# First loads cut by k and cast on two engines, warm-ups on a constant, and rows added into two banks throughout the last pass

## The reference

```python
s = jnp.einsum('bn,hln->bhl', x, beta)
ssq = jnp.einsum('bn,hln->bhl', x * x, beta * beta)
fm = 0.5 * jnp.sum(s * s - ssq, axis=-1)
linear_out = x @ W.T + b
return fm + linear_out
```

## Time and profile before

| | us |
|---|---|
| median of 3 runs | 778.99 (777.09 to 779.22) |
| profiled execution, its own time | 776.45 |
| its span, first to last instruction | 774.7 |
| PE busy in the span | 770.4 |
| DVE busy in the span | 570.5 |

### The profile page before, as it was taken

How to read it: one execution, slowest core, us unless ns; L and a number is a source line. 1 busy time by engine, 2 the same in 40 slices (tenths; PEclk the granted TensorE clock), 3 DMA queues, 4 the chain that set the end, 5 groups by cost and what they waited for, 6 DMA issues and landing times.

```text
span 774.7 us, 9622 instructions
## 1 busy us (share of the span) xinstructions
PE 770.4 (99%) x3382; PEld 634.4 (82%) x3382; DVE 570.5 (74%) x582; ACT 395.9 (51%) x503; POOL 343.4 (44%) x264
## 2 busy tenths in 40 slices
PE   9999999999999999999999999999999999999998
PEld 6888888888888888888888888888888888888886
DVE  6898289958765876587658765876587658787776
ACT  6674356645554555455545554555455545553331
POOL 0144274345434643454345434643454357335332
PEclk9999999999999999999999999999999999999999
DMA  9697853185614660466046604650565056629833
GB/s 351 236 376 322 302 191 123 69 297 210 221 33 150 217 218 28 149 218 218 28 150 218 222 29 153 220 212 29 170 226 194 28 191 210 221 72 402 322 126 153
DMA packets 64160, 145.34 MB, mean 188 GB/s; under 512 B 4848, under 2 KB 41712, under 8 KB 61808
## 3 DMA queue, kind: packets, MB, share of 16 engines
q1 hardware_dynamic: 64112, 144.72, 52.2%
HBM read 102.76 MB, written 41.94 MB: 187 GB/s over the span
## 4 chain that ended last, share of the span: by engine, by line
PE 99%; ACT 0%; DVE 0%; issue 0%
PE bank L459 33%; PE bank L463 33%; PE bank L465 33%; PE bank L452 1%; PE bank L484 0%; PE bank L487 0%; PE bank L491 0%; ACT cs L718 0%; DVE r L722 0%
## 5 line engine op out<-in xcount | busy, mean ns | idle before, releaser
L463 PE MATMUL bank<-t_lo,s_hi 128*128 128x512 f32 x1116 | 434.1, 389 | 0.0
L459 PE MATMUL bank<-t_hi,s_hi 128*128 128x512 f32 x1108 | 431.4, 389 | 0.0
L465 PE MATMUL bank<-t_hi,s_lo 128*128 128x512 f32 x1108 | 431.0, 389 | 0.0
L463 PEld LDWEIGHTS bank<-t_lo,s_hi 128*128 128x128 f32 x1116 | 209.5, 188 | 43.4
L459 PEld LDWEIGHTS bank<-t_hi,s_hi 128*128 128x128 f32 x1108 | 208.0, 188 | 44.0 <-DVE cs L929 0.4
L465 PEld LDWEIGHTS bank<-t_hi,s_lo 128*128 128x128 f32 x1108 | 208.0, 188 | 43.2
L850 DVE TENSOR_REDUCE sums<-cs 128x256 f32<-128x2048 f32 x64 | 146.3, 2286 | 120.9 <-issue 86.4
L1008 POOL TENSOR_TENSOR r<-r 128x512 f32<-128x512 f32 x70 | 95.1, 1359 | 263.0 <-ACT r L641 263.0
L1012 POOL TENSOR_TENSOR cs<-r 128x512 f32<-128x512 f32 x70 | 93.9, 1341 | 116.8 <-issue 112.8
L649 ACT ACTIVATE cs<-bank 128x512 f32<-128x512 f32 x64 | 38.3, 598 | 204.5 <-PE bank L465 204.5
L726 DVE TENSOR_TENSOR t_lo<-t_lo_in,t_hi 128x1024 fp32r<-128x1024 f32 x63 | 107.1, 1704 | 0.0
(11 more groups left out here) (70 smaller groups left out, 318.1 us busy)
## 6 DMA issues: line engine op xcount, KB each, us to landing
s_hi<-s_hi_kept SPq DMA_DIRECT2D x30, 896.0 KB, 5.0
s_lo<-s_lo_kept SPq DMA_DIRECT2D x30, 896.0 KB, 6.9
t_lo_in<-beta_p SPq DMA_DIRECT2D x16, 1024.0 KB, 7.2
s_lo_in<-x_p SPq DMA_DIRECT2D x17, 512.0 KB, 5.4
acc_kept<-cs SPq DMA_DIRECT2D x16, 512.0 KB, 5.0
acc<-acc_kept SPq DMA_DIRECT2D x64, 128.0 KB, 5.4
acc_kept<-acc SPq DMA_DIRECT2D x64, 128.0 KB, 1.8
s_hi_kept<-s_hi SPq DMA_DIRECT2D x8, 896.0 KB, 6.1
```

The lines of the kernel that those rows point to most:

```text
L459: nc.tensor.matmul(to, s_hi[:, slot, s_op, cols], hi[:, k, :], start=start, stop=False, skip_group_check=True)
L463: nc.tensor.matmul(to, s_hi[:, slot, s_op, cols], lo[:, k, :], start=False, stop=False, skip_group_check=True)
L465: return nc.tensor.matmul(to, s_lo[:, slot, s_op, cols], hi[:, k, :], start=False, stop=stop, skip_group_check=True)
```

## The change

**Start.** A new array `first_p` holds, for each k, the k slices of group 0's A11 and A21 and of B11 side by side. It comes in two DMAs of 384 KB (`first_loaded[k]`), into part of `cs`. Then follow A11 and A21 of group 1 (256 KB), B12 (512 KB), the other x blocks of both groups in one DMA (512 KB), and, after a wait for the second of the first loads, B21 and B22. The blocks of x are stored in the order A11, A21, A12, A22. DVE casts the k = 0 slice of B11 itself, while ACT casts x. PE goes through the first products by k (`first_parts`), both banks in turn: hi hi, lo hi, hi lo. The products with B12 come second and those with B21 third. Nine warm-ups in place of ten read a constant 1.0, with no wait. The order of the later casts, sums and copies of the start is rewritten to match.

**Last pass.** Groups 73 to 78 are handled like group 79: DVE adds the old rows into banks E and D (not A) after it has read P5 and P7, PE's P3 and P4 wait for `e_raised` and `d_raised`, and the last sums take r2. POOL's two adds are left only in group 72.

```diff
+
+A11, S4, A12, A22, S1, S2, S3 = range(OPS)
 A21 = S4
...
-            load_x_part(0, slice(0, 2), x0_front_loaded)
-            load_first(B11, b11_loaded)
-            load_x_part(0, slice(2, 4), x0_rest_loaded)
-            load_x_part(1, slice(0, 4), x1_loaded)
+            for k in range(KP):
+                sp.dma_start(first[:, k, 0:2 * P + COLS], first_p[k]).then_inc(first_loaded[k], 16)
+            sp.dma_start(s_lo_in[:, 1, 0:2, :].rearrange("p b c -> p (b c)"), x_p[1][:, 0:2 * KP * P]
+                         ).then_inc(x_second_loaded, 16)
+            load_first(B12, b12_loaded)
+            sp.dma_start(s_lo_in[:, 0:DIRECT, 2:4, :].rearrange("p g b c -> p g (b c)"),
+                         x_p[0:DIRECT, :, 2 * KP * P:].rearrange("g p c -> p g c")).then_inc(x_rest_loaded, 16)
+
+            sp.wait_ge(first_loaded[KP - 1], 16)
             load_first(B21, b21_loaded)
-            load_first(B12, b12_loaded)
             load_first(B22, b22_loaded)
...
-            pe.wait_ge(warm_up_ready, 1)
+            ones = nc.const_aps.tensor(1.0, [P, COLS], bf16)
             for _ in range(WARM_UP):
-                nc.tensor.matmul(banks[-1][:, :], warm_up[:, 0:P], warm_up, start=True, stop=True)
+                nc.tensor.matmul(banks[-1][:, :], ones[:, 0:P], ones, start=True, stop=True)
...
+            def first_parts(g, k):
+
+                cols = slice(k * P, (k + 1) * P)
+                hi, lo = t_hi[:, 0, B11, k, :], t_lo[:, 0, B11, k, :]
+                place = X_FIRST_PLACE + k if g == 0 else X_SECOND_PLACE
+                pe.wait_ge(s_hi_ready, place)
+                pe.wait_ge(first_hi_ready if k == 0 else t_hi_ready, 1 + k)
+                for bank_at, s_op in ((BANK_A, A11), (BANK_D, A21)):
+                    nc.tensor.matmul(bank(g, bank_at), s_hi[:, g, s_op, cols], hi,
+                                     start=k == 0, stop=False, skip_group_check=True)
+                pe.wait_ge(s_lo_ready, place)
+                for bank_at, s_op in ((BANK_A, A11), (BANK_D, A21)):
+                    nc.tensor.matmul(bank(g, bank_at), s_lo[:, g, s_op, cols], hi,
+                                     start=False, stop=False, skip_group_check=True)
+                pe.wait_ge(t_lo_ready, 1 + k)
+                for bank_at, s_op in ((BANK_A, A11), (BANK_D, A21)):
+                    nc.tensor.matmul(bank(g, bank_at), s_hi[:, g, s_op, cols], lo,
+                                     start=False, stop=k == KP - 1, skip_group_check=True)
+
+
+            for g in range(DIRECT):
                 for k in range(KP):
-                    cols = slice(k * P, (k + 1) * P)
...
-            first_product(0, BANK_A, A11, 1)
-            first_product(0, BANK_D, A21, 2)
-            first_product(1, BANK_A, A11, 3)
-            first_product(1, BANK_D, A21, 3)
-            for g in range(DIRECT):
-                whole(g, BANK_A, A12, B21, False).then_inc(direct_made, 1)
-                whole(g, BANK_D, A22, B21, False).then_inc(direct_made, 1)
+                    first_parts(g, k)
             for g in range(DIRECT):
                 for place, s_op in ((BANK_E, A11), (BANK_B, A21)):
                     for k in range(KP):
                         product(bank(g, place), g, s_op, t_lo[:, 1, T2, :, :], t_lo[:, 1, T3, :, :], k,
                                 k == 0, k == KP - 1, B12_SPLIT_PLACE)
+            pe.wait_ge(s_lo_ready, X_REST_PLACE)
+            for g in range(DIRECT):
+                whole(g, BANK_A, A12, B21, False).then_inc(direct_made, 1)
...
-                if g == GROUPS - 1:
-                    pe.wait_ge(e_raised, 1)
+                    pe.wait_ge(e_raised, g - FIRST_Q)
                 whole(g, BANK_E, S4, B22, False).then_inc(p3_made, 1)
                 if g <= FIRST_Q:
                     pe.wait_ge(r7_copied, count(g))
                 else:
                     pe.wait_ge(p7_taken, g - FIRST_Q)
-                if g == GROUPS - 1:
-                    pe.wait_ge(d_raised, 1)
+                    pe.wait_ge(d_raised, g - FIRST_Q)
...
-            act.wait_ge(x0_front_loaded, 16)
-            split_x(0, slice(0, 2))
-            act.wait_ge(b11_loaded, 16)
-            for k in range(KP):
-                split_high(0, B11, slice(k, k + 1))
-            act.wait_ge(x0_rest_loaded, 16)
-            split_x(0, slice(2, 4))
-            act.wait_ge(x1_loaded, 16)
-            split_x(1, slice(0, 4))
+            act.wait_ge(first_loaded[0], 16)
+            split_first_x(0)
+            act.wait_ge(first_loaded[1], 16)
+            split_first_x(1)
+            nc.scalar.copy(t_hi[:, 0, B11, 1, :], first_b11(1)).then_inc(t_hi_ready, 2)
+            act.wait_ge(x_second_loaded, 16)
+            nc.scalar.copy(s_hi[:, 1, 0:2, :], s_lo_in[:, 1, 0:2, :]).then_inc(s_hi_ready, 1)
+            act.wait_ge(b12_loaded, 16)
+            nc.scalar.copy(t_lo[:, 1, T2, :, :], t_at(0, B12)).then_inc(t_hi_ready, 1)
+            act.wait_ge(x_rest_loaded, 16)
+            nc.scalar.copy(s_hi[:, 0:DIRECT, 2:4, :], s_lo_in[:, 0:DIRECT, 2:4, :]).then_inc(s_hi_ready, 1)
             act.wait_ge(b21_loaded, 16)
             split_high(0, B21)
-            act.wait_ge(b12_loaded, 16)
-            nc.scalar.copy(t_lo[:, 1, T2, :, :], t_at(0, B12)).then_inc(t_hi_ready, 1)
+            act.wait_ge(first_t_summed, t_sum_place(0, T1))
+            split_high(0, T1)
             act.wait_ge(b22_loaded, 16)
             split_high(0, B22)
+            split_high(0, T3)
+            act.wait_ge(first_t_summed, t_sum_place(0, T2))
+            split_high(0, T2)
             copy_direct(0)
             copy_direct(1)
-            act.wait_ge(first_t_summed, t_sum_place(0, T1))
-            split_high(0, T1)
+            split_s(2)
             copy_direct(2)
             copy_direct(3)
-            act.wait_ge(first_t_summed, t_sum_place(0, T2))
-            split_high(0, T2)
-            split_high(0, T3)
             act.wait_ge(first_t_summed, t_sum_place(0, T4))
             split_high(0, T4)
-            split_s(2)
-            copy_direct(4)
-            copy_direct(5)
+            for number in range(4, 8):
+                copy_direct(number)
             split_s(3)
-            copy_direct(6)
...
-            nc.vector.memset(warm_up, 0.0).then_inc(warm_up_ready, 1)
...
+            dve.wait_ge(first_loaded[0], 16)
+            nc.vector.tensor_copy(t_hi[:, 0, B11, 0, :], first_b11(0)).then_inc(first_hi_ready, 1)
+            split_first_x(0)
+            split_first_b11(0)
+            split_first_x(1)
+            split_first_b11(1)
+            dve.wait_ge(s_hi_ready, X_SECOND_PLACE)
+            nc.vector.tensor_tensor(s_lo[:, 1, 0:2, :], s_lo_in[:, 1, 0:2, :], as_f32(s_hi[:, 1, 0:2, :]),
+                                    ALU.subtract).then_inc(s_lo_ready, 1)
             dve.wait_ge(t_hi_ready, B12_SPLIT_PLACE)
             nc.vector.tensor_tensor(t_lo[:, 1, T3, :, :], t_at(0, B12), as_f32(t_lo[:, 1, T2, :, :]),
                                     ALU.subtract).then_inc(t_lo_ready, 1)
-            split_low(0, B22)
+            dve.wait_ge(s_hi_ready, X_REST_PLACE)
+            nc.vector.tensor_tensor(s_lo[:, 0:DIRECT, 2:4, :], s_lo_in[:, 0:DIRECT, 2:4, :],
+                                    as_f32(s_hi[:, 0:DIRECT, 2:4, :]), ALU.subtract).then_inc(s_lo_ready, 1)
+            split_low(0, B21)
+            dve.wait_ge(b22_loaded, 16)
             sum_t(0, T3, B22, B12)
             dve.wait_ge(first_t_summed, t_sum_place(0, T3))
             dve.wait_ge(t_lo_ready, B12_SPLIT_PLACE)
-            sum_t(0, T1, B12, B11)
+            nc.vector.tensor_tensor(t_at(0, T1), t_at(0, B12),
+                                    first[:, :, 2 * P:2 * P + COLS],
+                                    ALU.subtract).then_inc(first_t_summed, 1)
             dve.wait_ge(first_t_summed, t_sum_place(0, T1))
             sum_t(0, T2, B22, T1)
             split_low(0, T1)
+            split_low(0, B22)
+            sum_s(2)
+            split_low(0, T3)
             dve.wait_ge(first_t_summed, t_sum_place(0, T2))
             sum_t(0, T4, B21, T2)
+            split_s(2)
             split_low(0, T2)
-            split_low(0, T3)
-            sum_s(2)
             split_low(0, T4)
-            split_s(2)
             sum_s(3)
...
+            def take_p5(g):
+                f = f_at(g - FIRST_Q)
+                dve.wait_ge(f_loaded[g - FIRST_Q], 16)
+                dve.wait_ge(p5_made, count(g))
+                nc.vector.tensor_tensor(f[:, 1, COLS:], bank(g, BANK_E), f[:, 1, COLS:], ALU.add
+                                        ).then_inc(p5_taken, 1)
+                nc.vector.tensor_tensor(bank(g, BANK_E), bank(g, BANK_E), f[:, 0, COLS:], ALU.add
+                                        ).then_inc(e_raised, 1)
+
+            def take_p7(g):
+                f = f_at(g - FIRST_Q)
+                dve.wait_ge(p7_made, count(g))
+                dve.wait_ge(p5_taken, g - FIRST_Q)
```

(95 more changed lines are left out.)

87 lines of the change are left out of this document (31 added, 56 removed).

## The result

The changed kernel takes 775.26 us by the median of 9 runs (775.0 to 776.27), the kernel before 777.15 us by 9 runs of the same comparison (776.5 to 780.06). The ratio is 0.9972, 95% interval 0.9961 to 0.9983: 2.2 us, clear of no change and just inside the 0.3% that the forecast used as its line. The time lies in the stated range, at its lower end; 777.4 was 2.1 us too high.

What follows compares the result with a forecast made beforehand. The prediction took PE's matmuls, 0.2266 us each, to bound the kernel. Start 1.2 plus last pass 0.35 made 1.55 us, taken from 778.99 for 777.4 us; the eight-in-ten range was 775.2 to 779.2 us.

Steps and rivals of the forecast that it cites:

- What bounds the kernel: Whole run: PE's matmuls at 0.2266 us each fill it; only about 1.5 to 2 us are lost, at start and last pass.
- The last pass: Groups 73 to 79: DVE's group falls from 9.75 to 9.44 us, below PE's 9.52, and the lost 0.35 us comes back.
- The slower rival: Last pass: DVE's waits for POOL turn into others, its group takes 10.95 us, the kernel 786.0 us; chance 0.06.
- The first operands: Start: first loads land at 3.7 and 4.84 us, first hi hi is ready at 4.5, just under the warm-ups' 4.6.
- What comes behind: Start, after the first operands: later loads, casts and subtractions are ready before PE wants them, at no cost.
- The later loads land by bytes, too: Start: B12 lands at 7.5 us, the other x at 8.8, B22 at 11.3, group 1's x some 5.8.
- These edits I cost at nothing: Start: later operands are covered by PE's own matmuls; B12 has the thinnest cover, 0.2 us.
- the start's 1.2 us: Start: the gain taken, as the middle of 0.8 to 1.7 us for different clock rises.
- 0.3 for this case: Start, clock up at 4.6 us or before: 0.3 us of waits, 25th matmul at 10.3, gain 1.7 us.
- The base: Whole run: the time the gain was subtracted from, the runs' median of 778.99 us; the profiled execution had 776.45.
- The one that gave the other runs of before a greater loss than the profiled one: Start: other runs' clock rises some 3 us later, so 1.4 us more are won, giving 776.0 us; chance 0.25.
- the sum at the start: Start: the 25th matmul's time follows from the clock's rise, 0.47 us per us of low clock; gains 0.8 to 1.7 us.

Runs made afterwards that it cites:

- after_again: The changed kernel run once more with no edit, with a second profile of its start: 775.05 us, ratio to the kernel before 0.9968.
- after_third: The changed kernel run a further time with no edit, as the measure of another call: 775.54 us, ratio to the kernel before 0.9977.
- start_only: The changed kernel with the last pass of the kernel before: 775.92 us, ratio to the kernel before 0.9976.

## Why the prediction was right or wrong

**What bounds the kernel.** Right: between start and last pass nothing changed (674.9 to 675.1 us from the 49th real matmul to the marker in six profiles), and the gain is made of the two places named.

**The last pass.** Right in size: 0.35 us, as forecast. Group 73's spare time was right too: L948 at 707.56, the add into E done at 708.85, P3 at 709.19, 0.34 us. DVE's group, estimated at 9.44 us, measured 8.18. The prediction kept two waits of before that went with the others, 0.8 us of the difference of 1.26; the rest are smaller gaps between DVE's instructions:

```profile
716.12 0.83 DVE L801 TENSOR_TENSOR s_lo_in<-s_lo_in 128x256 f32<-128x256 f32 x1
...
719.85 2.03 DVE L813 TENSOR_TENSOR s_lo<-s_lo_in,s_hi 128x1792 fp32r<-128x1792 f32 x1 [0.37 <-ACT s_hi L608]
```

L801, next to POOL's last add, is L805 in the changed kernel and takes 0.41 us there; the wait for ACT's cast is filled by the add into D. The slower rival needed a group of more than 9.52 us and was never near.

**The first operands.** The loads landed at 3.81 and 4.79 (forecast 3.7 and 4.84). DVE's cast took 0.43 us, not the 0.69 of its bound. The first real matmul came at 4.39, not 4.6, and at 4.31 and 4.41 in the other two profiles, about 0.15 us behind the end of that cast each time, whether the clock was high by then (`after_again`) or not (`after_third`).

**What comes behind: the step that failed.** "The later loads land by bytes, too" and, with it, "These edits I cost at nothing" took the landing times of one execution for those of any. B12 (1536 KB in all) was put at 7.5 us; it landed at 9.06, 8.70 and 8.84 in the three profiles of the changed kernel, and the same bytes land at 8.40 to 9.04 in the other four profiles with the loads of before: the 7.48 that was read is the earliest of all. Group 1's x was put at 5.8; it came at 7.08, 7.41 and 6.16, since the DMA rate dips between 4 and 6.5 us. The term mis-sized by this is the start's 1.2 us, and it erred on both sides. The changed start of the first profile, though its clock was high from the second real matmul on, lost 1.5 us between the 1st and the 49th (12.37 us for 48 x 0.2266), where the sum had 0.3 for this case: its marker is only 0.7 us earlier than that of the first profile of before. And the loads that are late cost the kernel before more, as it needs 1.0 MB for its 7th and 1.5 MB for its 13th matmul, the changed kernel for its 13th and 25th. Between the typical executions the start is worth 2.0 us by the landing-to-marker times, for the same landing, 1.5 by the means of three markers each (692.39, 693.74 and 693.06 with the start of before, 691.69, 691.57 and 691.46 of the changed kernel), and 1.9 (1.2 to 2.5) by the ratio of `start_only`. Why the rate dips stays open.

**The base.** The sum was taken from 778.99 us, a median of 3 runs; over 9 it is 777.15. That is 1.8 of the 2.1 us by which 777.4 was too high; the rest is what the start gained beyond the sum. From the profiled execution's own base, 776.45, the sum gave 774.9, and the changed kernel's profiled execution took 775.58: a gain of 0.9 us, for the base was a lucky one.

**The rivals.** The one that gave the other runs of before a greater loss than the profiled one had the right effect and, in the main, the wrong mechanism: not a later clock, but later loads. The range holds 775.26 only because of this rival's price, which was worked out from the clock; that part is luck. The spread of 776.45 to 779.22 had shown that one execution did not stand for the kernel, so 0.25 for it was low. The clock was also put into the sum at the start as what decides the gain, and the table above shows the marker following the loads instead. When it rises is random here: with warm-ups that begin at 1.19 in both, by the steps it rose near 7.25 in the first profile of before and by 4.1 in the second. This agrees with what the Trainium skill says (TensorE: Matmul & The Clock Gate, Part 1), though the difference is 3 us and not half a us. What part of before's wide spread is a clock that rises late stays open.

## What to carry to other kernels

At a start, count the bytes that must have landed before the n-th matmul, and order both loads and products so that this count stays low; here, moving the loads alone only moved the wait. A landing time from one profile is one draw: take a second profile of the kernel before, or the spread of its runs, before a fraction of a microsecond is read from it. A DVE add into the bank that PE will add to next takes a POOL step out of the loop, and here it cost PE nothing, as it ended 0.34 us before PE came back to the bank.
